# Two SiLUs behind both tiles' gates, per-piece waits for the last weight, and new engine orders in a two-layer transformer kernel

## What is computed

```python
x = x + L0_xattn(layernorm(x), ctx)   # one head: softmax(q k^T) of the context with itself, applied to x
x = x + L0_ffn(layernorm(x))          # activations quantised to 8 bits, weights ternary:
                                      # h -> (value, gate), u = value * silu(gate), out = u @ w_out^T; returns h_in + out
x = x + L1_xattn(layernorm(x), ctx)   # 16 heads over the context, 8 key/value heads, softmax, output projection
x = x + L1_ffn(layernorm(x))          # weights rounded to fp8: silu(gate) * up, then down; inner width 768
```

## Time and profile before

| | us |
|---|---|
| median of 3 runs | 320.16 |
| lowest, highest | 319.19, 320.66 |
| the profiled execution, its own time | 319.45 |
| its span, first to last instruction | 317.4 |
| TensorE busy | 294.9 |
| ScalarE busy | 258.5 |
| VectorE busy | 252.2 |
| GpSimd busy | 217.9 |

### The profile page before, as it was taken

How to read it: one execution, slowest core, us unless ns; L and a number is a source line. 1 busy time by engine, 2 the same in 40 slices (tenths; PEclk the granted TensorE clock), 3 DMA queues, 4 the chain that set the end, 5 groups by cost and what they waited for, 6 DMA issues and landing times.

```text
span 317.4 us, 6401 instructions
## 1 busy us (share of the span) xinstructions
PE 294.9 (93%) x1981; PEld 258.8 (82%) x1992; DVE 252.2 (79%) x713; ACT 258.5 (81%) x607; POOL 217.9 (69%) x290
## 2 busy tenths in 40 slices
PE   3676999999999999999989999999999999999994
PEld 2465566889988987899779989889999998989784
DVE  3789698989888789888889788897877595766674
ACT  0869796489999989999997897788899998975350
POOL 3786663566887788797877897878897696772001
PEclk9999799999999999999999999999999999999999
DMA  7994602002046867678637566687665466200201
GB/s 219 380 350 135 176 0 68 1 1 76 5 81 179 245 168 199 165 209 202 180 88 207 150 179 162 165 221 203 147 188 151 116 197 200 69 2 0 68 1 66
DMA packets 54609, 44.59 MB, mean 140 GB/s; under 512 B 11696, under 2 KB 45104, under 8 KB 54576
## 3 DMA queue, kind: packets, MB, share of 16 engines
q1 hardware_dynamic: 54016, 43.93, 49.1%
q10 hardware_dynamic: 560, 0.26, 0.3%
HBM read 27.01 MB, written 15.20 MB: 133 GB/s over the span
## 4 chain that ended last, share of the span: by engine, by line
PE 21%; ACT 15%; POOL 8%; issue 5%; DVE 1%; ACTq 0%; POOLq 0%; DVEq 0%
PE pb L2015 14%; PE pb L2278 4%; ACT sm L980 4%; POOL tp_lo L666 4%; ACT pT_hi L992 3%; PE pb L2312 2%; POOL xn L588 1%; ACT sm L998 1%; ACT L980 1%; POOL sm L661 1%; ACT L1019 1%; ACT fuse L1019 1%; ACT q_hi L975 1%; ACT oT_hi L1004 1%; POOL rstd L582 1%
## 5 line engine op out<-in xcount | busy, mean ns | idle before, releaser
L666 POOL TENSOR_TENSOR tp_lo<-tp,pT_hi 128x512 fp32r<-128x512 f32 x54 | 69.2, 1297 | 20.9 <-ACT pT_hi L992 20.8
L980 ACT ACTIVATE sm<-sm,smin 128x256 f32<-128x256 f32 x128 | 63.6, 503 | 1.1 <-DVE smin L1563 0.7
L1563 DVE CUSTOM_DVE_ANT_0 sm<-pb,mask_all 128x256 f32<-128x256 f32 x128 | 47.5, 419 | 4.0 <-PE pb L2015 3.6
L1580 DVE STREAM_TRANSPOSE blocks<-sm 128x1024 f32<-128x1024 f32 x27 | 33.5, 1240 | 7.0 <-DMA block_room<-blocks 6.1
L2015 PE MATMUL pb<-ctx_hi,q_hi 128*128 128x256 f32 x128 | 37.8, 295 | 0.5 <-DVE q_lo L1550 0.4
L2015 PE MATMUL pb<-xT_hi,m_hi 128*128 128x256 f32 x128 | 37.2, 291 | 0.1
L2015 PE MATMUL pb<-n_hi,oT_hi 128*128 128x256 f32 x128 | 37.1, 290 | 0.1
L2015 PE MATMUL pb<-xT_hi,m_lo 128*128 128x256 f32 x128 | 36.2, 283 | 0.0
L2015 PE MATMUL pb<-xT_lo,m_hi 128*128 128x256 f32 x128 | 36.2, 283 | 0.0
L2015 PE MATMUL pb<-ctx_hi,q_lo 128*128 128x256 f32 x128 | 36.2, 282 | 0.0
L2015 PE MATMUL pb<-ctx_lo,q_hi 128*128 128x256 f32 x128 | 36.1, 282 | 0.0
(11 more groups left out here) (195 smaller groups left out, 946.4 us busy)
## 6 DMA issues: line engine op xcount, KB each, us to landing
block_room<-blocks SPq DMA_DIRECT2D x108, 128.0 KB, 2.5
tp<-block_room SPq DMA_DIRECT2D x54, 256.0 KB, 3.1
w_raw<-in_w SPq DMA_DIRECT2D x4, 576.0 KB, 4.2
wraw<-in_wgvT SPq DMA_DIRECT2D x4, 512.0 KB, 7.4
wraw<-in_woutT SPq DMA_DIRECT2D x2, 512.0 KB, 10.6
out<-xb SPq DMA_DIRECT2D x4, 256.0 KB, 2.2
xa<-in_x SPq DMA_DIRECT2D x3, 256.0 KB, 4.6
xb<-in_ctxT SPq DMA_DIRECT2D x2, 256.0 KB, 6.1
```

Source lines behind the costliest of these rows:

```text
L666: g.tensor_tensor(tp_lo[:, z, c, :], tp[:, z, c, :], as_f32(pT_hi[:, c, :]), ALU.subtract).then_inc(pT_lo_pool, 1)
L980: a.activation(sm[:, n % 2, k, :], sm[:, n % 2, k, :], ACT.Exp, bias=smin[:, n % 2, k:k + 1], scale=-1.0, accum_out=ssum[:, n % 2, k:k + 1 ...
L1563: v.tensor_tensor_reduce(out=sm[:, n % 2, k, :], in0=bank(passing_bank("s", 2 * n + h))[:, (k % 2) * S:(k % 2 + 1) * S], in1=mask_all[:, b ...
L1580: v.transpose(blocks[:].rearrange("p g k b -> p k g b"), sm[:, n % 2, :, :].rearrange("p k (g b) -> p k g b", b=32)).then_inc(blocks_done, 1)
```

## The change

Three things, in one diff. First, on ScalarE `silu(j)` becomes `silus(b)`, which waits for all four gate halves of a batch and issues the calls for both of its tiles behind each other; it is called for batches 2 and 3:

```diff
-            def silu(j):
-                act.wait_ge(gate_done, 2 * (j - 2 * TB) + 2)
-                act.wait_ge(gsc_done, j // TB + 1)
-                a.activation(su[:, j % 2, :], su[:, j % 2, :], ACT.Silu, scale=gsc[:, j:j + 1]).then_inc(silu_done, 2)
+
+            def silus(b):
+                act.wait_ge(gate_done, 4 * (b - 2) + 4)
+                act.wait_ge(gsc_done, b + 1)
+                for j in range(TB * b, TB * (b + 1)):
+                    a.activation(su[:, j % 2, :], su[:, j % 2, :], ACT.Silu, scale=gsc[:, j:j + 1]).then_inc(silu_done, 2)
```

Second, `down(c, n)` of the first half of the tokens waits for the pieces that hold its own rows of the weight:

```diff
                 pe.wait_ge(f_lo_done, c + 1)
+                if c < KI:
+                    pe.wait_ge(w8_done, -(-(2 * KD * INNER + (i + 1) * D) // PIECE))
                 if c == 0 and n == 0:
-                    pe.wait_ge(w8_done, B * EIGHTS)
                     left, count = left_bank(last_passing(3))
```

```diff
-            projected1(0)
             context_high(0)
+            projected1(0)
             values_high(0)
+            sums(0)
             rows1(0)
             exps1(0)
             projected1(1)
-            sums(0)
             sums(1)
             probs1(0)
-            rows1(1)
             exps1(1)
```

and at the end of the second attention:

```diff
             contexts(27, 1)
+            attn_out(26, 0)
+            up4(4)
+            attn_out(26, 1)
             scores(31, 0)
-            scores(31, 1)
-            attn_out(26, 0)
-            attn_out(26, 1)
             contexts(28, 0)
-            up4(4)
             contexts(28, 1)
             down(0, 1)
             down(1, 1)
+            attn_out(27, 0)
+            scores(31, 1)
             down(2, 1)
-            attn_out(27, 0)
             attn_out(27, 1)
```

More of the change, by code:

```diff
@@ L251, in xattn_ffn_kernel @@
         ABS_ACT, ABS_DVE = (1, 3, 5), (0, 2, 4)
[L254 to L262, removed]
[7 rows of a table removed]
-                   ("gate", 10, 0), ("s", 13, 7), ("q", 7, 1), ("gate", 11, 3), ("rows", 1, 2), ("ctx", 3, 0), ("s", 14, 3),
-                   ("s", 15, 4), ("q", 8, 5), ("q", 9, 2), ("q", 10, 4), ("s", 16, 7), ("s", 17, 1), ("ctx", 4, 7),
-                   ("s", 18, 1), ("s", 19, 2), ("value", 9, 1), ("ctx", 5, 5), ("value", 10, 2), ("value", 11, 0), ("s", 20, 3),
[3 rows of a table removed]
-                   ("s", 29, 7), ("out", 4, 0), ("out", 5, 2), ("ctx", 10, 3), ("value", 12, 0), ("rows", 2, 5), ("s", 30, 4),
[16 rows of a table removed]
@@ L1135, in _ @@
             queries(6)
-            silu(4)
             normalise(5)
-            outputs(2)
             gate_copy(5, 0)
+            gate_copy(5, 1)
+            silus(2)
             probs(3, 0)
             queries(7)
-            gate_copy(5, 1)
             probs(3, 1)
+            rows3(1)
             exps(6, 0)
-            rows3(1)
             exps(6, 1)
+            probs(4, 0)
+            normalise(6)
             outputs(3)
-            normalise(6)
-            probs(4, 0)
-            probs(4, 1)
             queries(8)
@@ L1161, in _ @@
             queries(10)
+            normalise(8)
             exps(9, 0)
-            exps(9, 1)
-            normalise(8)
+            outputs(5)
             probs(6, 0)
             probs(6, 1)
-            silu(5)
+            exps(9, 1)
             exps(10, 0)
+            queries(11)
+            outputs(6)
             probs(7, 0)
-            outputs(5)
             normalise(9)
@@ L1199, in _ @@
             probs(10, 0)
+            normalise(13)
             probs(10, 1)
+            gate_copy(7, 0)
             outputs(9)
-            silu(6)
+            gate_copy(7, 1)
             queries(15)
-            gate_copy(7, 1)
-            normalise(13)
-            silu(7)
+            silus(3)
+            probs(11, 0)
             outputs(10)
-            probs(11, 0)
             exps(14, 0)
@@ L1266, in _ @@
             exps(22, 0)
+            rows4(0)
+            rows3(3)
             exps(22, 1)
-            normalise(21)
-            rows3(3)
             outputs(18)
@@ L2602, in _ @@
             attn_out(21, 1)
+            scores(27, 0)
+            queries(28)
+            scores(27, 1)
+            up4(0)
+            queries(29)
+            contexts(23, 0)
             scores(28, 0)
             scores(28, 1)
[L2605 to L2606 removed]
             contexts(23, 1)
+            queries(30)
             attn_out(22, 0)
[L2609 to L2610 removed]
             attn_out(22, 1)
[L2612 removed]
             contexts(24, 0)
```

842 lines of the change are left out of this document (424 added, 418 removed), and 52 rows, old and new, of the table PASSING.

## The result

The changed kernel takes **323.97 us** (median of 4 runs, 322.11 to 324.95), the kernel before on the same chip 319.96 (319.19 to 320.66): a ratio of **1.0117, 95% interval 1.0084 to 1.0151**. It is slower by about 3.7 us; forecast were 3.0 us less. The time lies outside the range and on its other side. The profiled execution took 323.51, its span is 321.5 (before 317.4).

What follows compares the result with a forecast made beforehand. TensorE, 93% busy, bounds the kernel: it waits in the head, shares 75 to 160 us with a full ScalarE, then is full alone. Gains 1.0 + 0.5 + 1.5 = 3.0 us give median 317.2 us, range 314.0 to 320.6.

Steps and rivals of the forecast that it cites:

- The rest of the head's order: Head up to 40 us: reordered TensorE and SP work only fills gaps; 0.5 us gain, bounds loss 1 to gain 2.5.
- The head's ScalarE and SP order: Head: context copy first and sums(0) ahead of exp bring first exp to about 11.0 from 12.00; 1.0 us gain.
- The paired SiLU: 75 to 160 us: paired SiLU blocks drop two ScalarE table loads, 2.57 us; 1.5 us gain taken.
- D: Rival: table loads don't go, ScalarE keeps 16, only the head's 1.0 to 1.5 us is left; 318.9 us, chance 0.05.
- C: Rival: pair's block starves TensorE, a contexts(3,0) or contexts(11,0) wait exceeding some 1.5 us; slower, 322.3 us, chance 0.12.
- Waits per piece: Downs from 274.40 us: each waits only for its own row's pieces, the sixteenth done ahead of need; cost 0.
- tail: From last attention output to end: same work in another mixture, scores(31,1) later but covered with 1.2 us room; cost 0.
- The orders from 75 us on: Orders of 160 to 290 us not priced singly: between a gain of 1 and a loss of 1.5 us, taken as 0.

Runs made afterwards that it cites:

- c: Kernel before with only context_high(0) moved ahead of projected1(0) on ScalarE: 318.53 us, ratio 0.9975.
- csp: Kernel before with context_high(0) first on ScalarE and SP's new order up to turn_rows(2): 318.44 us, ratio 0.9968.
- f: Changed kernel with ternary(0) put back ahead of probs1(1) on ScalarE: 320.63 us, ratio to before 1.0031.
- h2f: New head with the old rest and unpaired SiLUs, and ternary(0) ahead of probs1(1) on ScalarE: 322.14 us, ratio to before 1.0086.
- d: Changed kernel plus 24 unread transposes on TensorE, 14 ahead of probs(2), 10 ahead of the first gate: 319.46 us, ratio to before 1.0014.
- p1: Kernel before with only the first SiLU pair, silus(2), behind gate_copy(5, 1): 321.26 us, ratio 1.0066.
- p: Kernel before with only the pairing, silus(2) and silus(3): 323.66 us, ratio 1.0132.
- h1: Changed kernel with every engine's orders and banks up to about 75 us as before: 320.62 us, ratio to before 1.0043.
- h2: Changed kernel's orders up to about 75 us, then those of before with unpaired SiLUs: 322.73 us, ratio to before 1.0099.
- g: Old head with context_high(0) first and SP's new order, then the new rest with paired SiLUs: 320.05 us, ratio to before 1.0022.
- s: Changed kernel with SP's old order behind turn_rows(2): 326.87 us, ratio to before 1.0240.

## Why the prediction was wrong

**The step that failed is "The rest of the head's order"**, priced as "This only fills gaps", 0.5 us to the good with a loss of 1 as the bound. Measured, the new head costs 2.3 to 3.2 us although its chain gained about 1 (c, csp), so this step cost 3 to 4, as the milestones above say too. Two things were missed. First, I counted which work moved ahead, and not which ready work now stood behind a wait: ternary(0) behind probs1(1) on ScalarE. "Most can't be won" was right, but a list can also lose. By f this swap is 2.7 of the 3.7 us in the changed kernel, by h2f only 0.5, within the noise, ahead of the old rest; inverse1(2) behind weight_sums(1) on VectorE is not shown to matter. Second, I took a stall to be worth its length. The earlier trace rows already had a granted clock of 0.96 for the stage up to 40 us, and the prediction didn't read the column. The new stall of 1.70 us was followed by some 7 us at half clock in which mix(2) alone took 1.7 us more than at full. How the 3 to 4 us divide between late work and the clock stays open; d, which fills the stalls and keeps the clock, takes 3.3 away.

*The head's ScalarE and SP order*, 1.0: right. The first exp at 11.12 as forecast (11.6 on average over the profiles), 0.8 and 1.0 us in kernels that change this alone. Its lead was lost some 20 us later, at probs(2).

*The paired SiLU*, 1.5: the loads went as counted (two, 2.57 us), D fell, and the cover held: the longest wait is 0.7 us, so C's condition wasn't met; the kernel is slower for another reason than C's. Its mechanism is real in the old order. C worked out 2.3 us a block and took 2.6 off for the loads, 2.1 for both; p1 and p measured 2.1 for one and 4.2 for both with the saved loads in it, so nothing came off, and part of p's is the clock's. The gain was 0.1 in the changed kernel and 1.2 and 1.6 where TensorE isn't late: the term was right for a kernel that doesn't exist as long as the head is late. Terms of one path don't add when one of them moves the engine that the other relieves. As for the drain that the Trainium skill, "ScalarE: Activation LUTs", section "What ACT_TABLE_LOAD costs", puts at each switch: in the changed kernel a copy ends at 101.87, the load starts at 101.93 and the SiLUs at 103.22, when it ends. The trace still doesn't agree.

*Waits per piece* and *tail*, 0: right. Neither wait appeared.

*The orders from 75 us on*, 0 between +1 and -1.5 to the good: by h1 and h2 a cost of 0.5 to 1.4 with the pairing in it, inside the bound. Without the pairing the orders cost 0.2 and 0.6 behind the new head and 2.9 behind the old one with the context first (g, csp), outside it. Which lists do it was not separated; SP's is not the one (s).

The sum should have read -1.0 for the chain, +3 to +4 for the rest of the head, 0 for the pairing, +0.5 to +1.4 for the rest. The 13% for slower were too few above all because the only rival on that side was a stall in the middle; the head, where the order of all engines changed most, had only a bound of 1 for a loss and no rival.

## What to carry to other kernels

When an order written by hand changes, go through each engine's list for ready work that now stands behind a wait, not only for work that moved ahead. Read the granted clock beside TensorE's busy share in every stage: time lost to half clock counts as busy, and a stall of under 2 us can cost more than its length. Price a saving on a second engine only after the first one's arrival in that stage is settled: here the same edit was worth 0.1, 1.2 or 1.6 us, or cost 2.1 for one block alone, by what surrounded it. Filling a stall of TensorE with useless work helps only where it really stands still: the same filler in front of ready work cost 2.4 us.

## What was not expected of the hardware

ScalarE's first table load needs no input: with the copy of the context first in the list it ran at 2.21 us, under the wait for the DMA, where the earlier trace rows has it at 7.51 behind a wait for TensorE. All profiles with the copy first have it at 2.20 to 2.24.

Useless work made a kernel faster: 24 transposes, 3.0 us of TensorE's rows, brought 3.3 us. The same ones cost the kernel before 2.4 us, half of whose runs read 1.0 without them and half with them.

A low share of work on TensorE isn't always followed by half clock. h1's profile has TensorE busy 0.90, 1.12 and 1.10 us in the windows of 2 us from 28 to 34, all at clock 1.00, the middle one

```profile
30.00:32.00 2.00, 1.12 (x11) 0.88 (x9) 1.93 (x9) 2.00 (x4) 0.78 (x1) 1.00 0.34 87
```

and five of its 11 runs read clock 1.0, four 0.989. The kernel before is of the same kind: 15 of 32 runs at 1.0, six at 0.989. Every profile of the changed head without the transposes has the stretch. What decides it between equal programs stayed open.
